# Adding pairs of heads' gates on GpSimd, so that TensorE's sums take two matmuls in place of four

## The reference

```python
    sim = jnp.einsum('pbthn,hkpn->pbthk', q, keys)
    scores_xy, idx_xy = jax.lax.top_k(sim, K)
...
    all_scores = (sx[..., :, None] + sy[..., None, :]).reshape(b, t, h, K * K)
...
    scores, pk = jax.lax.top_k(all_scores, K)
    indices = jnp.take_along_axis(all_idx, pk, axis=-1)
    de = down_embed[indices]
    ue = up_embed[indices]
    w = jax.nn.silu(jnp.einsum('btd,bthkd->bthk', hidden_states, de) * jax.nn.softmax(scores, axis=-1))
    experts_states = jnp.einsum('bthk,bthkd->btd', w, ue)
    dense = jnp.einsum('bti,di->btd', jax.nn.silu(jnp.einsum('btd,id->bti', hidden_states, W_up)), W_down)
    return dense + experts_states
```

## Time and profile before

| | |
|---|---|
| Median of three runs | 1496.2 us (1495.67 to 1496.87) |
| The profiled execution | 1500.2 us, its span 1498.9 us |
| Busy in the span | TensorE 1258.3 us (84%), VectorE 967.3 (65%), ScalarE 623.6 (42%), GpSimd 423.1 (28%) |
| L917, sums of gates | 512 records of matmuls, 275 ns each in the median, the first at 238.8 us and the last at 507.7 us |

### The profile page before, as it was taken

One profiled execution on the slowest core, in us unless ns is written; L12 is line 12 of the kernel. 1 busy time (PEld: TensorE's weight loads), 2 busy tenths in 40 slices (PEclk: granted clock), 3 DMA queues, 4 the chain that ended last, 5 costly groups with the idle time before them and its releaser, 6 DMA issues.

```text
span 1498.9 us, 23059 instructions
## 1 busy us (share of the span) xinstructions
PE 1258.3 (84%) x8094; PEld 828.3 (55%) x8094; DVE 967.3 (65%) x2897; ACT 623.6 (42%) x1625; POOL 423.1 (28%) x691
## 2 busy tenths in 40 slices
PE   5377669888988579999999999999999998577885
PEld 3266625555555446656666665566566665265555
DVE  3588777888876347766666566566666665365465
ACT  1000024444444235555555555555555554412331
POOL 1013241333313124343343333333433433101010
PEclk9598989999999769999999999999999999778797
DMA  6200020000000000000000000000000000000000
GB/s 181 78 1 1 1 85 1 1 1 1 1 1 1 0 0 1 1 2 1 1 1 2 1 1 1 1 1 1 1 1 1 1 1 1 0 3 5 8 8 8
DMA packets 18402, 15.33 MB, mean 10 GB/s; under 512 B 2416, under 2 KB 16752, under 8 KB 18160
## 3 DMA queue, kind: packets, MB, share of 16 engines
q1 hardware_dynamic: 18288, 13.86, 3.1%
HBM read 12.81 MB, written 1.05 MB: 9 GB/s over the span
## 4 chain that ended last, share of the span: by engine, by line
PE 62%; DVE 19%; ACT 9%; issue 7%; POOL 1%; SPq 0%; DMA 0%; DVEq 0%; ACTq 0%; POOLq 0%
PE bank L1395 11%; PE bank L1439 10%; PE bank L1405 8%; PE bank L1596 4%; ACT prb L1464 4%; PE bank L917 3%; PE bank L1349 3%; PE bank L1727 2%; PE bank L1380 2%; DVE negmax L1544 2%; DVE moe L1788 2%; PE bank L1372 2%; PE bank L1399 2%; PE bank L1359 2%; PE bank L902 2%
## 5 line engine op out<-in xcount | busy, mean ns | idle before, releaser
L1490 POOL TENSOR_SCALAR prb<-prb,rnorm 128x512 f32<-128x512 f32 (+3 forms) x512 | 272.5, 549 | 477.9 <-DVE rnorm L1561 475.7
L1464 ACT ACTIVATE prb<-bank,negmax 128x512 f32<-128x512 f32 (+3 forms) x512 | 264.4, 525 | 288.1 <-DVE negmax L1544 283.9
L1544 DVE TENSOR_REDUCE negmax<-bank 128x1 f32<-128x512 f32 (+3 forms) x512 | 219.2, 480 | 126.6 <-PE bank L1399 124.9
L1395 PE MATMUL bank<-kT,qT 64*128 64x512 f32 (+3 forms) x1024 | 202.2, 479 | 3.2 <-ACT prb L1464 3.2
L1405 PE MATMUL bank<-ident,prb 128*128 128x128 f32 x1280 | 193.0, 282 | 3.0 <-POOL prb L1490 1.9
L1405 PEld LDWEIGHTS bank<-ident,prb 128*128 128x128 f32 x1280 | 141.4, 142 | 49.5 <-issue 24.9
L1439 PE MATMUL bank<-prbT,vv 128*64 128x512 f32 (+3 forms) x1024 | 151.9, 439 | 1.7 <-issue 0.8
L1552 DVE COPY prbT<-bank 128x512 f32<-128x512 f32 x128 | 87.7, 685 | 87.0 <-PE bank L1405 87.0
L1395 PEld LDWEIGHTS bank<-kT,qT 64*128 64x128 f32 x1024 | 77.8, 186 | 52.7 <-issue 37.5
L1464 ACT ACTIVATION_READ_ACCUMULATOR prb<-bank,negmax 128x1 f32 x512 | 102.2, 200 | 0.0
L1439 PEld LDWEIGHTS bank<-prbT,vv 128*64 128x64 f32 x1024 | 63.8, 136 | 67.7 <-issue 60.4
(11 more groups left out here) (438 smaller groups left out, 2126.8 us busy)
## 6 DMA issues: line engine op xcount, KB each, us to landing
ew2T<-in_ew2T SPq DMA_DIRECT2D x1, 1024.0 KB, 6.4
ew<-in_ew SPq DMA_DIRECT2D x1, 1024.0 KB, 5.7
wq<-in_Wq SPq DMA_DIRECT2D x2, 512.0 KB, 4.9
wk<-in_Wk SPq DMA_DIRECT2D x2, 512.0 KB, 7.0
wv<-in_Wv SPq DMA_DIRECT2D x1, 1024.0 KB, 7.9
out<-res SPq DMA_DIRECT2D x16, 64.0 KB, 1.5
wmod<-in_wmod SPq DMA_DIRECT2D x2, 384.0 KB, 3.9
c_filt_sb<-in_c_filt SPq DMA_DIRECT2D x1, 768.0 KB, 7.0
```

Of the source, the lines that this page charges most:

```text
L1395: T.matmul(s_of(j, s, i, qc), q[r, qc * P:(qc + 1) * P], k[r, 0:(qc + 1) * P], start=True, stop=False)
L1464: A.activation(prb[j % 2][:, i, p_at[qc]:p_at[qc] + (qc + 1) * P], s_of(j, s, i, qc), ACT.Exp, bias=negmax[j % 2][:, place[qc], i:i + 1], ...
L1490: last = G.tensor_scalar(v, v, rnorm[j % 2][:, place[qc], i:i + 1], 1.0, ALU.mult, ALU.mult)
L1544: V.tensor_reduce(negmax[j % 2][:, place[qc], i:i + 1], s_of(j, s, i, qc), AX.X, ALU.max, negate=True).then_inc(at_max, 1)
```

## The change

GpSimd gets a function `halve(n)`. It waits for both silus of tile n, and adds heads 2 and 3 of `prob` to heads 0 and 1 in place: one addition of 128 x 1024 in f32. `sums(n)` waits for it with the new semaphore `ff_halved`, and sums two heads with 8 matmuls in place of 16. The last matmul, for `past_sum`, is as before. At each odd n, `halve(n-1)` stands within `past_of(n+1)`, between `chosen_past` and the first product of `zpast`, and `halve(n)` behind `past_of(n+1)`. At n = 15 there is no `past_of(16)`, and both stand at the end.

```diff
@@ sums(n), TensorE
                 T.wait_ge(ff_past, n + 1)
-                T.wait_ge(ff_w, 2 * n + 2)
+                T.wait_ge(ff_halved, n + 1)
                 for c in range(EXPERTS // P):
-                    for h in range(PH):
+                    for h in range(PH // 2):
                         last = T.matmul(SUMS[:, c * P:(c + 1) * P], prob[n % 3][:, h, c * P:(c + 1) * P], ident[:, :],
-                                        start=(h == 0), stop=(h == PH - 1 and c < 3))
+                                        start=(h == 0), stop=(h == PH // 2 - 1 and c < 3))
@@ feed_forward_gpsimd
+            def halve(n):
+                G.wait_ge(ff_w, 2 * n + 2)
+                p = prob[n % 3]
+                G.tensor_tensor(p[:, 0:2, :], p[:, 0:2, :], p[:, 2:4, :], ALU.add).then_inc(ff_halved, 1)
+
@@ past_of(n), behind chosen_past
+                if n >= 2 and n % 2 == 0:
+                    halve(n - 2)
                 pool.settle()
                 G.wait_ge(ff_epair, n + 1)
@@ the loop over n
                 if n + 1 < TILES:
                     past_of(n + 1)
+                elif n % 2:
+                    halve(n - 1)
+                if n % 2:
+                    halve(n)
```

More of the change, by code:

```diff
@@ L331, in build @@
         (ff_up, ff_silu, ff_sim, ff_simk, ff_best, ff_apart, ff_ebest, ff_epair, ff_chosen, ff_code, ff_rsum, ff_zpast, ff_turned, ff_codeT, ff_rank,
-         ff_mask, ff_logit, ff_prob, ff_gd, ff_past_gate, ff_z, ff_past, ff_w, ff_sums, ff_wT, ff_out, ff_res) = (sem("ff_" + n) for n in (
+         ff_mask, ff_logit, ff_prob, ff_gd, ff_past_gate, ff_z, ff_past, ff_w, ff_halved, ff_sums, ff_wT, ff_out, ff_res) = (sem("ff_" + n) for n in (
              "up", "silu", "sim", "simk", "best", "apart", "ebest", "epair", "chosen", "code", "rsum", "zpast", "turned", "codeT", "rank",
-             "mask", "logit", "prob", "gd", "past_gate", "z", "past", "w", "sums", "wT", "out", "res"))
+             "mask", "logit", "prob", "gd", "past_gate", "z", "past", "w", "halved", "sums", "wT", "out", "res"))
         dve_own, act_own, pool_own = sem("dve_own"), sem("act_own"), sem("pool_own")
```

## The result

The changed kernel takes 1504.87 us in the median of seven runs (1503.4 to 1510.17), the kernel before 1496.96 beside it. The ratio is 1.0047, with a 95% interval of 1.0027 to 1.0067: slower by about 7 us (the two medians are 7.9 apart). The profiled execution took 1506.87 us, its span is 1505.5.

What follows compares the result with a forecast made beforehand. No engine is saturated; the chain of waits within a feed-forward pair bounds the stage. 7 x (-1.10) - 1.5 + 1.0 = -8.2, plus 6.0 for clock falls, gives -2.2 us: 1498.0 profiled, 1494.0 measured; range 1487 to 1502.

Steps and rivals of the forecast that it cites:

- With four of seven gaps falling: +6.0: TensorE's idle times before each pair's first sums: the clock falls in four of seven, at 1.5 us each, +6.0 us.
- falls in all: Rival, chance 0.20: the clock falls in six or seven pairs; seven at 1.5 us give +2.3 us, 1498.5.
- five of eight gaps: In the old trace, TensorE fell from 2.4 to 1.2 GHz in five of eight stretches beginning with such a gap.
- this costs nothing by itself: TensorE's wait before `down` for VectorE's gates, ending about 0.15 us later: free, since ScalarE's chain does not pass there.
- The price: Cost of one clock fall behind the first sums' gap: between 1.3 and 2.6 us, taken as 1.5.
- blocking: GpSimd holding VectorE: `ebest` +1.0 us in the sum; as a rival, also first `halve` behind `xeq`, 1496.4, chance 0.12.
- The last pair: Tiles 14 and 15: fewer matmuls against late first and last sums, together about -1.5 us.
- The add: GpSimd's `halve`, one 128x1024 f32 addition per tile: 2.35 us, from a line through other sizes, ends 1.96 and 2.53.
- -1.10 a pair without the clock: Per pair: sums of n-1 wait for their add, +0.69 us; sums of n have it covered, -1.79 us.
- The gap of 2.2 us: TensorE's idle time before each pair's first sums grows from 1.00 to 2.2 us, 3.5 in the first pair.
- The hidden things: Later zpast products and normalisation behind GpSimd's adds delay nobody; zpast has 6 us to spare.
- VectorE at its limit: VectorE had only 0.51 us idle before its second-half gate; it ends its gates about 0.15 us later.

Runs made afterwards that it cites:

- the kernel with 8 spare matmuls: The changed kernel plus 8 useless identity matmuls on TensorE before the wait for the add, first tile of each pair only: 1494.28 us, ratio 0.9967.

## Why the prediction was wrong

The range ended at 1502.0; the time is 1504.9, and slower had a chance of 0.20. The forecast step that failed is "With four of seven gaps falling: +6.0", in both of its factors. The outcome was the case "falls in all", chance 0.20, at a price that the range left out: it stopped at 2.0 us a fall, though the prediction's own row of 2.64 gave +10.3.

- *How often.* The clock fell in each of the seven pairs, where I counted five of eight gaps at other places, and left the one at 490.62, which fell too, out of the count. In six pairs it fell at the gap in front of the first sums, which recurs at 2.25 to 2.5 us with the same work around it; in the experiments the five pairs from n = 3 on held up to 1.82 us and fell from 1.87 on. In the seventh it fell in an idle time of 2.36 us in front of `down`, at 458, where the kernel before has 1.48 and kept its clock. For this idle time the prediction had "this costs nothing by itself". In the experiments 1.48 us fell there and 2.37 held (the rows in front of "The last pair"), so that no length decides at every place. The three gaps that had held stood in other surroundings; what set them apart was not tried. The rival "falls in six or seven pairs" was the outcome, and a wait that recurs in each period and lowers the clock in every one, as the Trainium skill (TensorE: Matmul & The Clock Gate, HAM oscillation — how this bites in real kernels) describes it, is what the pairs from n = 3 on show. But the waits of the case in that section are about 3 to 5 us long. The waits of 3.42 us with the add for even tiles alone are of that length, and the trace agrees with it there, five of five; those of the changed kernel were 2.25 to 2.53, and for them the section supported the rival less than the prediction has it.
- *The price.* I took 1.5 us from short falls, and had 2.6 as the upper bound. Against the kernel with 8 spare matmuls the first five pairs are longer by 3.6, 2.5, 1.65, 1.4 and 2.6 us, in the mean 2.4. It follows how long the clock stayed low: 3.4 us cost 1.4 to 1.65, 6.8 us 2.5 to 2.6, and 10.2 us 3.6, a third to a half of the low time. The experts and the code behind the sums, which I counted in part or not at all, ran at half speed as well. The bound of 2.6 was too low.
- *The sum by places.* From the first sums of the first pair to those of the last the forecast had -0.7 us, and it was 255.3 before and 262.8 after, +7.5. That is 8.2 us too many. With the -1.10 a pair taken off, the seven pairs lost 15.2 us, 2.2 each, where the forecast had 7.0 for clock and blocking together; the sixth and seventh lost less than the five above, 1.6 and 1.4. (The seventh had 6.8 us at low clock before the change, too.) Blocking, at +1.0 for `ebest`, was over-counted.
- *The last pair*, -1.5: wrong by about 3.4 us. From its first sums to the transposes behind (L853 at 516.56 and 522.33) it took 22.5 us before and 21.9 after, for a forecast of 18.5. The clock stayed low for 17.1 us there, with idle times of 5.87 and 1.44 us, and `x<-x,gated`, held by `halve(15)`, kept `dense(15)` waiting for 1.44 us.
- *Not of the change:* the first sums of the first pair start at 237.64, 1.2 us earlier than before though an add stands in front of them, for which the forecast had +2.5. The time up to there, almost all of it untouched by the change, has a mean clock of 0.88 in place of 0.85; +7.5, -0.6 and -1.2 make the 5.8 us by which the stage ends later. That was luck: without it the forecast would have been 3.6 us further off.
- *The add*, 2.35 us: right (2.354). The straight line through rows of other sizes was good to 0.01 us; the estimate of 2.25 from the Trainium skill (GPSIMD Engine Reference, Elementwise — side-by-side cycle accounting) was 0.1 short.
- *-1.10 a pair without the clock, made of +0.69 and -1.79:* right: 35.70 for 36.72 (-1.02), +0.64 for the first add alone and -1.65 for the second.
- *The gap of 2.2 us, 3.5 in the first pair:* right, 2.25 to 2.53 and 3.45.
- *The hidden things:* nobody waited for zpast, nor for the normalisation within the pairs (TensorE waits for it 13.5 us in two places outside them, before and after alike). *VectorE at its limit:* right; `down` waits 0.85 us for its last gate at 309.51, off ScalarE's chain.
- *`ebest` held for 0.2 us in five pairs:* wrong, see below.

## What to carry to other kernels

When a change puts a recurring wait of about 2 us in front of TensorE, price it as the wait plus a third to a half of a low stretch of 3 to 10 us, and expect the fall in every round rather than in some: of the waits of 2.03 us and more in the five like pairs, fifteen of fifteen fell. It isn't certain at a place of another kind, where 2.37 and 3.23 us held. Work that is handed from engine to engine on the critical chain is better cut into the pieces in which it is used: four adds of 0.72 us with the sums behind each were 16 us faster than the kernel before, one add of 2.35 us was 7 slower. And look at the two places of such a change one by one: the add whose result is needed 6 us later was worth 1.65 us a pair alone.

## What the runs showed of the hardware

VectorE's and GpSimd's blocking has two faces, here in the third pair, VectorE first:

```profile
320.72 1.96 DVE L1210 TENSOR_TENSOR x<-x,gated 128x128 f32<-128x128 f32 x1
...
326.45 0.18 DVE L1164 TENSOR_TENSOR ebest<-best 128x32 f32<-128x32 f32 x1
```

```profile
320.17 2.36 POOL L1070 TENSOR_TENSOR prob<-prob 128x1024 f32<-128x1024 f32 x1 [4.17 <-ACT prob L1017]
...
323.67 3.19 POOL L1064 TENSOR_SCALAR xhat_post<-x,mv_post,rstd_post 128x128 f32<-128x128 f32 x4
```

`x<-x,gated`, two operands in SBUF, starts at 320.72 beside the add and takes 1.96 us in place of 0.29: it ends 0.15 us behind the add. It is so at each of 14 starts beside a GpSimd operation of two tensors in this trace:

```profile
L1210 DVE TENSOR_TENSOR x<-x,gated x16: 291/886/1957, 244.9 to 516.2; 128x128 f32<-128x128 f32 x16
```

`ebest`, also with two operands in SBUF, starts at 326.45 inside one of the normalisation's four pieces (one tensor and two scalars a row) and takes its 0.18 us. Three starts of four beside such a piece were free like this one, the fourth (at 210.97) took 0.37. The Trainium skill (SBUF — State Buffer, Who interferes with whom) lets such an operation contend with any GpSimd instruction that reads SBUF; for one that reads two tensors the trace agrees, for this one it does not. The first adds hold VectorE as well: in the changed kernel `xeq` took 2.44 us at 460.87 where it takes 0.28 alone. That `x<-x,gated` cost nothing before the last pair is argued from VectorE's waits behind it (1.52 us here at 324.20), not tried.
